# Attention that transposes the scores before the exponential, takes every fourth query row as a tile, and sums the weights by columns of ones

## The chip, the core and the metric

The kernel runs on one core of one Trainium2 chip. The time is the device time of one execution in microseconds: 3637.33 us in the median of three runs (3631.33 to 3641.29). Engines are named as in the profile: PE multiplies matrices (PEld is its weight load), DVE, ACT and POOL do element work, SP only starts transfers. Sixteen DMA engines move data between the chip's memory (HBM) and SBUF; SP's transfers go through the hardware queue q1, POOL's through the software queue q0.

## The reference

The attention is that of 16 batches of 512 rows of 256 numbers, with 16 heads of 16 numbers each, and a relative-position term on both sides:

```python
scores = jnp.einsum('bhqd,bhkd->bhqk', q, k)
dist_idx = pos_l - pos_r + M - 1
pos_emb = dist_emb[dist_idx]
rel_q = jnp.einsum('bhld,lrd->bhlr', q, pos_emb)
rel_k = jnp.einsum('bhrd,lrd->bhlr', k, pos_emb)
scores = (scores + rel_q + rel_k) / jnp.sqrt(jnp.asarray(D, scores.dtype))
probs = jax.nn.softmax(scores, axis=-1)
ctx = jnp.einsum('bhqk,bhkd->bhqd', probs, v)
```

Around it stand a modulated layer norm, the projections, the output product and a mixture of 8 experts with 2 active.

## The kernel before, in words

`program` (near the end of the file) runs five stages one after the other, each a block in which every engine has its own written-out order: modulation, projections, distances, attention, experts. Only `attention` is touched.

The stage `distances` works out rel_q + rel_k for all 256 pairs of batch and head (called heads below) and writes them to HBM as `r_scratch`, 1 MB for each head, in blocks of 128 query rows l by 128 key rows. It loads `d_q` and `d_k` from POOL's queue to 48, 32 and 16 partitions at a time (L589).

The stage `attention` takes a head as four tiles of 128 query rows by 512 keys (TT = 4, tile L holds rows 128L to 128L+127). For one tile, PE makes the product q k (L893, a weight load of 128 columns of `qa`, `kb` moving), DVE adds the tile of r, multiplies by -0.25 and takes the row minimum in the same instruction (L977, `neg` and `low`), ACT takes the exponential with the row minimum as bias and sums it over the row (L1035, `e` and `total`), PE transposes `e` in four pieces (L903), and DVE (odd tiles, L985) or ACT (even tiles, L1042) copies the transposed weights from PSUM to `eT`. For each group of four heads PE multiplies `v` with `eT` (L914), DVE inverts the sums (L991), POOL spreads them (L820), PE transposes that (L924), ACT copies it to SBUF (L1048), DVE scales (L998), and POOL stores the context (L828).

The transfers: SP loads r, one transfer of 256 KB for each tile, into a ring of four heads (L860, `load_r`); a tile of the ring is loaded again when L977 has used it. `v` is loaded by SP for four heads at a time (L866). POOL loads `qa` and `kb` of a batch, which is 16 heads (L811, seven transfers to 48, 32 and 16 partitions, 3 MB in all), when the products of the batch before last are done.

Of the kernel before, what the change touches and what calls it, by code (L numbers as in the profile page):

```python
# [26 lines left out]
P = 128  # L27
# [692 lines left out]
def attention(nc, qf_d, ks_d, v_d, r_d, cT_d, nb=NB):  # L720
# [6 lines left out]
    with ctx:  # L727
# [13 lines left out]
        AHEAD = 2  # L741
        BANKS = 3
        SLOTS = 2 * H
        NH, NGR = nb * H, nb * H // GH
        BG = H // GH
        ident = sb("t_ident", [P, P])
        qa = sb("t_qa", [ROWS, 1, SLOTS, S], BF16)
# [3 lines left out]
        neg = sb("t_neg", [P, TT, S])  # L751
        low = sb("t_low", [P, 2, TT])
        e = sb("t_e", [P, 2, TT, S])
        total = sb("t_total", [P, 2, TT, GH])
        inv = sb("t_inv", [P, 2, TT, GH])
        wide = sb("t_wide", [P, TT * GH, CT])
        ones = sb("t_ones", [P, TT * GH])
        wideT = sb("t_wideT", [P, S])
        eT = sb("t_eT", [P, 2, GH, TT, TT, P])
        out = sb("t_out", [P, 2, S])  # L760
        tiny = sb("t_tiny", [P, 8])
        p_s = [ps(f"t_ps{i}", [P, S]) for i in range(BANKS)]
        p_t = [ps(f"t_pt{i}", [P, TT, P]) for i in range(BANKS)]
# [8 lines left out]
        r_loaded = [sem(f"t_r_loaded{i}") for i in range(RR * TT)]  # L772
        scored = sem("t_scored")
        added = sem("t_added")
        exped = sem("t_exped")
        turned = sem("t_turned")
        even_out = sem("t_even_out")
        odd_out = sem("t_odd_out")
        pc_zero = sem("t_pc_zero")
        weighed = sem("t_weighed")  # L780
        inverted = sem("t_inverted")
        widened = sem("t_widened")
        wide_turned = sem("t_wide_turned")
        wide_out = sem("t_wide_out")
        ctx_done = sem("t_ctx_done")
        ctx_stored = [sem(f"t_ctx_stored{i}") for i in range(2)]

        def bank(j, L):

            return (TT * j + L) % BANKS  # L790

        def since(j, L):

            i = TT * j + L
            return BANKS if i >= BANKS else next(k for k in range(1, 2 * BANKS) if (i - k) % (TT * U) % BANKS == i)

        with nc.Block() as block:
            @block.gpsimd
            def _(pool):
                nc.gpsimd.memset(ones[:], 1.0).then_inc(ident_zero, 1)  # L800
                nc.gpsimd.memset(ident[:], 0.0).then_inc(ident_zero, 1)
                pool.wait_ge(ident_zero, 2)
# [3 lines left out]
                def load(pair, u):  # L806
                    b = 2 * pair + u
                    g, b8 = b // GB, b % GB
                    for tensor, src, runs in ((qa, qf_d, A_RUNS), (kb, ks_d, B_RUNS)):
                        for row, stored, rows in runs:  # L810
                            pool.dma_start(tensor[row:row + rows, :, u * H:(u + 1) * H, :].rearrange("r n h w -> r n (h w)"),  # L811
                                           src[g, :, b8, stored:stored + rows, :, :].rearrange("n r h w -> r n (h w)")
                                           ).then_inc(batch_loaded[u], 16)

                def widen(G, par):

                    pool.wait_ge(inverted, G + 1)
                    later(pool, wide_turned, G)
                    narrow = inv[:, par].rearrange("p l j -> p (l j)").unsqueeze(2).to_broadcast([P, TT * GH, CT])
                    nc.gpsimd.tensor_tensor(wide[:], narrow, ones[:].unsqueeze(2).to_broadcast([P, TT * GH, CT]),  # L820
                                            ALU.mult).then_inc(widened, 1)

                def store(b, k):

                    pool.wait_ge(ctx_done, BG * b + k + 1)
                    for j in range(GH):
                        row = (GH * k + j) * D
                        pool.dma_start(cT_d[b, row:row + D, :], out[j * CT:j * CT + D, k % 2, :]  # L828
                                       ).then_inc(ctx_stored[k % 2], 16)

                def batch(pair, u, more=True):
                    b = 2 * pair + u
                    for k in range(BG):
                        if more or k + 1 < BG:
                            widen(BG * b + k + 1, (k + 1) % 2)
                        if more and k == BG - 1 and (not isinstance(pair, int) or b + 2 < nb):

                            pool.wait_ge(scored, TT * H * (b + 1))
                            load(pair + 1, u)
                        store(b, k)  # L840

                for u in range(2):
                    load(0, u)
                widen(0, 0)
                with pool.Fori(0, nb // 2 - 1) as pair:
                    for u in range(2):
                        batch(pair, u)
                for u in range(2):
                    batch(nb // 2 - 1, u, more=(u == 0))

                for par in range(2):
                    pool.wait_ge(ctx_stored[par], 16 * GH * NGR // 2)

            @block.sync
            def _(sp):
# [7 lines left out]
                def load_v(G, b, k):  # L863

                    later(sp, weighed, TT * (G - 1))
# [4 lines left out]
                def heads(g, b, half):  # L870

                    for j in range(U):
                        load_r(g, H * b + U * half + j, j)
                        if j % GH == GH - 1:
                            k = (U * half + j) // GH
                            load_v(BG * b + k, b, k)

                for half in range(2):
                    heads(0, 0, half)
                for g in range((nb + GB - 1) // GB):  # L880
                    with sp.Fori(max(1, g * GB), min((g + 1) * GB, nb)) as b:
                        for half in range(2):
                            heads(g, b, half)

            @block.tensor
            def _(pe):
                pe.wait_ge(ident_done, 1)
                pe.wait_ge(pc_zero, 1)

                def score(n, j, L, slot):  # L890

                    later(pe, added, TT * n + L - since(j, L) + 1)
                    nc.tensor.matmul(p_s[bank(j, L)][:], qa[:, 0, slot, L * P:(L + 1) * P], kb[:, :, slot, :],  # L893
                                     start=True, stop=True).then_inc(scored, 1)

                def turn(n, j, L):
                    t = TT * n + L

                    pe.wait_ge(exped, t + 1)
                    before = TT * j + L - since(j, L)  # L900
                    later(pe, (even_out, odd_out)[before % 2], TT // 2 * (n - j) + before // 2 + 1)
# [4 lines left out]
                def weigh(G, par, c, loads):  # L906
                    if c == 0:

                        pe.wait_ge(even_out, TT // 2 * GH * (G + 1))
                        pe.wait_ge(odd_out, TT // 2 * GH * (G + 1))  # L910
                        pe.wait_ge(v_loaded[par], 16 * loads)
                        later(pe, ctx_done, G)
                    for j in range(GH):
                        last = nc.tensor.matmul(p_c[j * CT:j * CT + D, :], vv[:, par, j, c, :],  # L914
                                                eT[:, par, j, c].rearrange("p l q -> p (l q)"),
# [3 lines left out]
                def turn_wide(G, L):  # L919
                    if L == 0:  # L920

                        pe.wait_ge(widened, G + 1)
                        later(pe, wide_out, G)
                    last = nc.tensor.transpose(p_i[:, L * P:(L + 1) * P],  # L924
# [693 lines left out]
```

## Time and profile before

| | |
|---|---|
| median of three runs | 3637.33 us |
| the profiled execution | 3640.87 us, its span 3639.3 us |
| mean granted clock of PE | 0.812 of full speed |
| busy: PE, DVE, ACT, POOL | 76%, 63%, 49%, 22% of the span |
| distances | about 366 to 1606 us |
| attention | about 1606 to 2870 us |
| HBM to and from the core | 848.79 MB, 233 GB/s over the span |

The page cuts the span into 40 slices of 91 us and gives the busy tenths of each engine, the granted clock and the bytes moved. A slice says that an engine was busy, not that it set the time; for that the waits are read. Attention is slices 18 to 31.

### The profile page before, as it was taken

To read this page: it belongs to the slowest core of one execution; us is meant where nothing else is said; L and a number is where in the kernel's file an instruction comes from. 1 tells how busy PE (TensorE), PEld (TensorE's weight loads), DVE (VectorE), ACT (ScalarE), POOL (GpSimd) and SP (SyncE) were. 2 spreads that over 40 slices of the span, in tenths; PEclk is the share of its full clock that TensorE was granted. 3 is DMA by queue.
4 is the path that set the end of the run, shared out by engine and by line. 5 is a ranking of instruction groups with operands and counts; after the bars stand their busy time and mean duration, and the time that the engine had idled before them with its cause. 6 is when DMAs were issued, how large, how long until landed. Compare 5 with 4: busy or idle time off the path is not lost. (4 is left out here: it accounts for less than half of the span.)

```text
span 3639.3 us, 69041 instructions
## 1 busy us (share of the span) xinstructions
PE 2756.1 (76%) x18124; PEld 1921.6 (53%) x18124; DVE 2294.1 (63%) x6133; ACT 1772.2 (49%) x3509; POOL 807.3 (22%) x907
## 2 busy tenths in 40 slices
PE   4665676776767767638878888878888688888887
PEld 2443576665766767635545555545555344444443
DVE  5664354554545545438877888878888666666664
ACT  2443453443534445318877888878888511111111
POOL 2442110111111111001211222212121224433334
PEclk7888575666766667659888999989999889999999
DMA  4999898979889799899999999999999711111110
GB/s 114 226 221 209 183 358 314 340 289 334 330 312 365 291 345 338 325 292 279 264 254 268 270 274 273 267 257 275 274 276 274 212 43 61 61 61 61 61 61 19
DMA packets 899306, 848.79 MB, mean 233 GB/s; under 512 B 236808, under 2 KB 809536, under 8 KB 864688
## 3 DMA queue, kind: packets, MB, share of 16 engines
q1 hardware_dynamic: 840112, 640.95, 60.2%
q0 software_dynamic: 59136, 207.14, 21.0%
q8 instruction: 28, 0.46, 0.1%
q14 instruction: 30, 0.25, 0.0%
HBM read 507.88 MB, written 340.05 MB: 233 GB/s over the span
## 5 line engine op out<-in xcount | busy, mean ns | idle before, releaser
L697 DVE TENSOR_TENSOR d_r<-d_pk,d_r 128x1024 f32<-128x1024 f32 x512 | 620.9, 1224 | 622.1 <-PE d_pk L654 487.9
L684 ACT ACTIVATE d_r<-d_pq 128x1024 f32<-128x1024 f32 x512 | 532.6, 1052 | 693.4 <-PE d_pq L643 686.9
L1035 ACT ACTIVATE t_e<-t_neg,t_low 128x512 f32<-128x512 f32 x1024 | 738.7, 734 | 231.5 <-DVE t_low L977 230.1
L643 PE MATMUL d_pq<-d_win,d_q 96*128 96x128 bf16 x4096 | 488.1, 278 | 303.1 <-DMA d_q<-q_chunks_scratch 283.4
L977 DVE CUSTOM_DVE_ANT_0 t_neg<-t_ps,t_r 128x512 f32<-128x512 f32 x1024 | 671.8, 687 | 28.4 <-issue 28.3
L903 PE MATMUL t_pt<-t_ident,t_e 128*128 128x128 f32 x4096 | 642.0, 280 | 1.5 <-DVE t_eT L985 0.6
L643 PEld LDWEIGHTS d_pq<-d_win,d_q 96*128 96x128 bf16 x4096 | 433.5, 193 | 327.8 <-issue 229.6
L893 PE MATMUL t_ps<-t_kb,t_qa 96*128 (+1 forms) x1024 | 405.0, 396 | 247.6 <-DVE t_low L977 182.5
L903 PEld LDWEIGHTS t_pt<-t_ident,t_e 128*128 128x128 f32 x4096 | 518.0, 145 | 110.9 <-ACT t_eT L1042 13.7
L654 PE MATMUL d_pk<-d_win,d_k 96*128 96x128 bf16 x4096 | 501.5, 288 | 76.6 <-DMA d_k<-k_chunks_scratch 45.1
L654 PEld LDWEIGHTS d_pk<-d_win,d_k 96*128 96x128 bf16 x4096 | 441.1, 187 | 105.0 <-DVE d_r L697 56.7
L1335 PE MATMUL e_pX<-e_we,e_h2T 128*128 128x512 f32 x1024 | 483.4, 623 | 0.8 <-DVE e_odd L1538 0.2
L985 DVE COPY t_eT<-t_pt 128x512 f32<-128x512 f32 x512 | 351.0, 686 | 2.4 <-PE t_pt L903 1.9
L893 PEld LDWEIGHTS t_ps<-t_kb,t_qa 96*128 (+1 forms) x1024 | 104.1, 102 | 436.6 <-issue 403.8
L1042 ACT ACTIVATE t_eT<-t_pt 128x512 f32<-128x512 f32 x512 | 307.3, 600 | 19.4 <-PE t_pt L903 19.3
L1335 PEld LDWEIGHTS e_pX<-e_we,e_h2T 128*128 128x128 f32 x1024 | 196.7, 198 | 227.3 <-issue 215.2
L914 PE MATMUL t_pc<-t_eT,t_v 128*16 128x512 f32 x2048 | 279.9, 620 | 0.9 <-DVE t_out L998 0.9
L820 POOL TENSOR_TENSOR t_wide<-t_inv,t_ones 128x512 f32<-128x512 f32 x64 | 66.7, 1042 | 787.3 <-DVE t_inv L991 787.3
L1035 ACT ACTIVATION_READ_ACCUMULATOR t_e<-t_neg,t_low 128x1 f32 x1024 | 215.3, 210 | 0.0
L596 POOL DMA_DIRECT2D d_win<-table_scratch x32 | 17.1, 533 | 841.3 <-PE d_pk L654 797.9
L976 DVE MEMSET t_tiny<- 128x1 f32 x1024 | 60.4, 59 | 226.7 <-DMA t_r<-r_scratch 114.2
L1530 DVE SCALAR_TENSOR_TENSOR e_even<-e_pX,e_mask,e_even 128x256 f32<-128x256 f32 x192 | 92.1, 480 | 169.6 <-ACT e_even L1405 101.7
(133 smaller groups left out, 2560.3 us busy)
## 6 DMA issues: line engine op xcount, KB each, us to landing
r_scratch<-d_r SPq DMA_DIRECT2D x256, 1024.0 KB, 18.4
t_r<-r_scratch SPq DMA_DIRECT2D x1024, 256.0 KB, 5.3
d_q<-q_chunks_scratch POOLq DMA_DIRECT2D x64, 768.0 KB, 16.0
d_q<-q_chunks_scratch POOLq DMA_DIRECT2D x64, 512.0 KB, 17.8
d_q<-q_chunks_scratch POOLq DMA_DIRECT2D x64, 256.0 KB, 19.6
t_kb<-k_chunks_scratch POOLq DMA_DIRECT2D x32, 512.0 KB, 20.3
q_chunks_scratch<-a_part SPq DMA_DIRECT2D x96, 128.0 KB, 3.6
q_rows_scratch<-a_part SPq DMA_DIRECT2D x96, 128.0 KB, 2.2
```

The lines of the kernel that those rows point to most:

```text
L643: last = nc.tensor.matmul(pq[n % 2][:, a, :], q[u][:, :, l % CW], rhs, start=True, stop=True)
L654: last = nc.tensor.matmul(pk[n % 2][:, a, :], k[u][:, :, c % CW], win[par][:, TB - 1 - c:2 * TB - 1 - c], start=True, stop=True)
L684: nc.scalar.activation(r[u][:, n * QL:(n + 1) * QL, :], pq[n % 2][:], ACT.Copy).then_inc(q_out, 1)
L697: nc.vector.tensor_tensor(part, pk[n % 2][:].rearrange("p r l -> p l r"), part, ALU.add).then_inc(k_added, 1)
L893: nc.tensor.matmul(p_s[bank(j, L)][:], qa[:, 0, slot, L * P:(L + 1) * P], kb[:, :, slot, :], start=True, stop=True).then_inc(scored, 1)
L903: last = nc.tensor.transpose(p_t[bank(j, L)][:, c, :], e[:, j % 2, L, c * P:(c + 1) * P], ident[:])
L914: last = nc.tensor.matmul(p_c[j * CT:j * CT + D, :], vv[:, par, j, c, :], eT[:, par, j, c].rearrange("p l q -> p (l q)"), start=(c == 0), ...
L977: nc.vector.tensor_tensor_reduce(out=neg[:, L, :], in0=p_s[bank(j, L)][:], in1=r[:, j % RR, L].rearrange("p c r -> p (c r)"), scale=-0.25, ...
L985: nc.vector.tensor_copy(eT[:, j // GH, j % GH, :, L, :], p_t[bank(j, L)][:]).then_inc(odd_out, 1)
L1035: nc.scalar.activation(e[:, j % 2, L, :], neg[:, L, :], ACT.Exp, bias=low[:, j % 2, L:L + 1], scale=-1.0, accum_out=total[:, j // GH, L, j ...
L1042: nc.scalar.activation(eT[:, j // GH, j % GH, :, L, :], p_t[bank(j, L)][:], ACT.Copy).then_inc(even_out, 1)
L1335: last = nc.tensor.matmul(pX[n][:], h2T[:, u, k, t * P:(t + 1) * P], we[:, k, n * 2 * E:(n + 1) * 2 * E], start=(k == 0), stop=(k == KC - 1))
```

## The change

Tile t of a head is now made of the query rows t, t+4, t+8, ... (every fourth), so that partition p holds the rows 4p to 4p+3 of a head. One partition's piece of r for one block of keys is then 2 KB without a gap in HBM, instead of four of 512 bytes. `load_r` brings a head in four transfers of 256 KB, as before, but each of them goes to 32 partitions and holds all four tiles (L875), where one went to 128 partitions and held one tile. A head of the ring is loaded again when all its four tiles are used.

The row minimum is subtracted in place: of tiles 0 and 1 by POOL, of tiles 2 and 3 by ACT. PE then transposes the scores, two tiles to a pair of PSUM banks, and ACT takes the exponential of both out of PSUM straight to `eT`, once for 128x1024 elements. DVE and ACT no longer copy transposed tiles. The sums are made by PE: `vx` holds `v` and 16 columns of ones, so the product has 32 rows for a head, and one of them, the sum, is picked by four small products with `pick`. The banks for the scores are two instead of three, and the weight load of the scores reads every fourth column. Loads of `qa` and `kb` and stores of the context move from POOL's queue to SP's.

```diff
+        vx = sb("t_vx", [P, 2, GH, TT, 2, D])
-        r = sb("t_r", [P, RR, TT, NT, TB])
+        r = sb("t_r", [P, RR, NT, TT, TB])
...
+                def subtract(n, j, t):
+
+                    pool.wait_ge(added, TT * n + t + 1)
+                    nc.gpsimd.tensor_scalar(neg[:, j % RING, t, :], neg[:, j % RING, t, :],
+                                            low[:, j % RING, t:t + 1], None, ALU.subtract).then_inc(pool_sub, 1)
...
                 def load_r(g, n, j):
-                    for L in range(TT):
-
-                        later(sp, added, TT * (n - RR) + L + 1)
-                        sp.dma_start(r[:, j % RR, L], r_d[g][L, :, n - g * P, 0:TB * TB].rearrange("c (l r) -> l c r", r=TB)
-                                     ).then_inc(r_loaded[j % RR * TT + L], 16)
...
+                    later(sp, added, TT * (n - RR + 1))
+                    for lc in range(NT):
+                        src = r_d[g][lc, :, n - g * P, 0:TB * TB].rearrange("c (p x) -> p c x", x=TT * TB)
+                        sp.dma_start(r[lc * P // NT:(lc + 1) * P // NT, j % RR].rearrange("p c t r -> p c (t r)"), src
+                                     ).then_inc(r_loaded[j % RR], 16)
...
+                    for j in range(H):
+                        load_r(g, H * b + j, j)
+                        k = j // GH
+                        if j % GH == 0:
+                            load_v(b, k)
+                        if j % GH == 1 and (not fixed or BG * b + k >= 3):
+                            store(b + (k - 3) // BG, (k - 3) % BG)
+                        if j == 4 and (not fixed or 1 <= b < nb - 1):
+                            nxt = pair + u
+                            load_next((b + 1) // GB if fixed else g, nxt, 1 - u)
...
+                def score(n, j, t):
+
+                    later(pe, added, TT * n + t - 1)
+                    lhs = qa[:, 0, n % SLOTS, :].rearrange("r (p t) -> r t p", t=TT)[:, t, :]
...
+                    if t < 2:
+                        pe.wait_ge(pool_sub, 2 * n + t + 1)
+                    else:
+                        pe.wait_ge(act_sub, 2 * n + t - 1)
+                    if t % 2 == 0:
+                        later(pe, exped, 2 * n + t // 2 - 1)
                     for c in range(TT):
-                        last = nc.tensor.transpose(p_t[bank(j, L)][:, c, :], e[:, j % 2, L, c * P:(c + 1) * P], ident[:])
+                        last = nc.tensor.transpose(p_t[t // 2][:, t % 2, c, :],
+                                                   neg[:, j % RING, t, c * P:(c + 1) * P], ident[:])
                     last.then_inc(turned, 1)
...
+                def sums(G, par):
+
+                    pe.wait_ge(emptied, G + 1)
+                    later(pe, scaled, G)
+                    for t in range(TT):
+                        last = nc.tensor.matmul(p_i[:, t * GH:(t + 1) * GH], cs[:, par, t * P:(t + 1) * P], pick[:],
+                                                start=True, stop=True)
+                    last.then_inc(summed, 1)
...
+                    nc.vector.tensor_tensor_reduce(out=neg[:, j % RING, t, :].rearrange("p (c r) -> p c r", r=TB),
+                                                   in0=p_s[t % 2][:].rearrange("p (c r) -> p c r", r=TB),
+                                                   in1=r[:, j % RR, :, t, :], scale=-0.25,
                                                    scalar=3.0e38, op0=ALU.add, op1=ALU.min,
-                                                   accum_out=low[:, j % 2, L:L + 1]).then_inc(added, 1)
-
-                def empty(n, j, L, G):
-
-                    dve.wait_ge(turned, TT * n + L + 1)
-                    later(dve, weighed, TT * (G - 1))
-                    nc.vector.tensor_copy(eT[:, j // GH, j % GH, :, L, :], p_t[bank(j, L)][:]).then_inc(odd_out, 1)
...
+                    nc.scalar.activation(neg[:, j % RING, t, :], neg[:, j % RING, t, :], ACT.Identity,
+                                         bias=low[:, j % RING, t:t + 1], scale=-1.0).then_inc(act_sub, 1)
...
+                    nc.scalar.activation(to, p_t[half][:], ACT.Exp, scale=(1.0 if half else -1.0)).then_inc(exped, 1)
```

In SP's queue, from the start of the stage, the rows before are these; "128x4x128" is partitions, key blocks and numbers in a run.

```order
L860 DMA t_r<-r_scratch 128x4x128 x16
L866 DMA t_v<-v_scratch 128x256
L860 DMA t_r<-r_scratch 128x4x128 [waits t_added] x16
L866 DMA t_v<-v_scratch 128x256
L860 DMA t_r<-r_scratch 128x4x128 [waits t_added] x16
```

After, in the same queue at the fifth and sixth head of batch 1, L866 is the load of the next batch's `qa` and `kb`, L891 a store of the context:

```order
L875 DMA t_r<-r_scratch 32x4x512 [waits t_added]
L875 DMA t_r<-r_scratch 32x4x512 x3
L882 DMA t_v<-v_scratch 128x256 [waits t_v_copied]
L866 DMA t_qa<-q_rows_scratch 48x8192 [waits t_scored]
L866 DMA t_qa<-q_rows_scratch 32x8192
L866 DMA t_qa<-q_rows_scratch 16x8192
L866 DMA t_kb<-k_chunks_scratch 16x8x1024 x2
L866 DMA t_kb<-k_chunks_scratch 32x8x1024 x2
L875 DMA t_r<-r_scratch 32x4x512 [waits t_added]
L875 DMA t_r<-r_scratch 32x4x512 x3
L891 DMA ctx_scratch<-t_out 16x512 [waits t_scaled]
```

The loads of r change shape, and the batch load now stands between the loads of r of two heads in one queue.

On ACT, in the steady order of heads before:

```order
L1042 ACTIVATE t_eT<-t_pt 128x4x128 [waits t_turned]
L1035 ACTIVATE t_e,t_total<-t_neg,t_low 128x512 [waits t_turned,t_added] x2
L1042 ACTIVATE t_eT<-t_pt 128x4x128 [waits t_turned]
L1035 ACTIVATE t_e,t_total<-t_neg,t_low 128x512 [waits t_turned,t_added] x2
L1042 ACTIVATE t_eT<-t_pt 128x4x128 [waits t_turned]
```

and after, where L1064 subtracts and L1074 is the exponential:

```order
L1064 ACTIVATE t_neg<-t_neg,t_low 128x512 [waits t_added]
L1074 ACTIVATE t_eT<-t_pt 128x2x4x128 [waits t_turned]
L1064 ACTIVATE t_neg<-t_neg,t_low 128x512 [waits t_added]
L1074 ACTIVATE t_eT<-t_pt 128x2x4x128 [waits t_turned]
L1080 ACTIVATE t_cs<-t_pc 128x512 [waits t_weighed]
```

A head is six instructions with four row sums before, and four without them now.

## Rows read from the trace of the kernel before

**Rows 1.** The page: busy tenths and GB/s in 40 slices.
```profile
PE   4665676776767767638878888878888688888887
PEclk7888575666766667659888999989999889999999
DMA  4999898979889799899999999999999711111110
GB/s 114 226 221 209 183 358 314 340 289 334 330 312 365 291 345 338 325 292 279 264 254 268 270 274 273 267 257 275 274 276 274 212 43 61 61 61 61 61 61 19
```

**Rows 2.** Waits of SP, 1632 to 2870: us in total, times, longest.
```profile
SPq L866 <- PE t_pc L914: 20.7, 22, 1.9
SPq L860 <- DVE t_low L977: 19.2, 32, 1.8
```

**Rows 3.** Waits of all engines, 1632 to 2870, same columns.
```profile
DVE t_tiny L976 <- DMA t_r<-r_scratch: 114.2, 24, 14.7
```

**Rows 4.** Timeline of SP, one batch: start, duration, transfers issued.
```profile
2031.73 13.49 SPq L860 DMA_DIRECT2D t_r<-r_scratch  x16
...
2047.30 32.90 SPq L860 DMA_DIRECT2D t_r<-r_scratch  x16
```

**Rows 5.** Transfers issued 2070 to 2120: count, size, us to landing.
```profile
t_r<-r_scratch SPq DMA_DIRECT2D x55, 256.0 KB, 5.2
```

**Rows 6.** Windows: length, busy PE, PEld, DVE, ACT, POOL, clock, DMA share, GB/s.
```profile
1606.00:2854.00 1248.00, 1022.83 (x7266) 632.10 (x7266) 990.98 (x3664) 997.73 (x2587) 248.83 (x422) 0.90 1.14 268
2000.00:2050.00 50.00, 49.90 (x376) 31.24 (x374) 49.95 (x187) 49.68 (x131) 14.38 (x25) 1.00 1.20 294
2050.00:2070.00 20.00, 6.73 (x51) 4.43 (x47) 6.28 (x25) 7.33 (x19) 0.54 (x2) 0.79 1.01 179
1990.00:1998.00 8.00, 7.38 (x34) 4.32 (x35) 5.46 (x21) 5.07 (x13) 1.04 (x1) 0.57 1.20 292
```

**Rows 7.** Instructions from 2000 to 2050: count, busy us, mean ns.
```profile
L977 DVE CUSTOM_DVE_ANT_0 t_neg<-t_ps,t_r 128x512 f32<-128x512 f32 x52 | 34.0, 687 | 0.0
```

**Rows 8.** Windows with POOL's transfers alone: 128 partitions, then 16 to 48.
```profile
58.00:60.00 2.00, 2.00 (x5) 0.76 (x4) 0.00 (x0) 1.08 (x2) 0.00 (x0) 0.99 0.93 311
366.00:400.00 34.00, 18.11 (x144) 15.46 (x144) 0.79 (x1) 15.86 (x16) 11.06 (x20) 0.50 0.99 160
```

**Rows 9.** Their packets, the first for 58 to 60, the second for 366 to 400.
```profile
q0 software_dynamic: 168, 0.62, 93.3%
q0 software_dynamic: 1507, 5.42, 99.0%
```

**Rows 10.** POOL's timeline, first loads of distances (48, then 32 partitions).
```profile
366.03 0.66 POOL L589 DMA_DIRECT2D d_q<-q_chunks_scratch  x1
366.89 2.86 POOL L589 DMA_DIRECT2D d_q<-q_chunks_scratch  x5 [0.20 <-issue]
```

**Rows 11.** Those two transfers: size, us from issue to landing.
```profile
d_q<-q_chunks_scratch POOLq DMA_DIRECT2D x1, 768.0 KB, 8.2
d_q<-q_chunks_scratch POOLq DMA_DIRECT2D x1, 512.0 KB, 10.0
```

**Rows 12.** The page's costliest groups: count, busy us, mean ns.
```profile
L684 ACT ACTIVATE d_r<-d_pq 128x1024 f32<-128x1024 f32 x512 | 532.6, 1052 | 693.4 <-PE d_pq L643 686.9
L643 PEld LDWEIGHTS d_pq<-d_win,d_q 96*128 96x128 bf16 x4096 | 433.5, 193 | 327.8 <-issue 229.6
L985 DVE COPY t_eT<-t_pt 128x512 f32<-128x512 f32 x512 | 351.0, 686 | 2.4 <-PE t_pt L903 1.9
L893 PEld LDWEIGHTS t_ps<-t_kb,t_qa 96*128 (+1 forms) x1024 | 104.1, 102 | 436.6 <-issue 403.8
L1042 ACT ACTIVATE t_eT<-t_pt 128x512 f32<-128x512 f32 x512 | 307.3, 600 | 19.4 <-PE t_pt L903 19.3
L820 POOL TENSOR_TENSOR t_wide<-t_inv,t_ones 128x512 f32<-128x512 f32 x64 | 66.7, 1042 | 787.3 <-DVE t_inv L991 787.3
```

**Rows 13.** Instructions of the attention stage, 1590 to 2910, same columns.
```profile
L924 PE MATMUL t_pi<-t_ident,t_wide 128*128 128x128 f32 x256 | 73.0, 287 | 0.0
```

More of the change, by code:

```diff
@@ new lines, in head @@
+                def head(step, j):
+                    n = U * step + j
+                    fixed = isinstance(n, int)
+                    if not fixed or n < NH:
+                        for t in range(2):
+                            subtract(n, j, t)
+                    if j % GH == 0 and (not fixed or 2 * GH <= n):
+                        widen(2 * step + j // GH - 2)
+                    if j % GH == 1 and (not fixed or n < NH):
+                        copy_v(step, j // GH)
+                for n in range(NH + GH + 1):
+                    head(n // U, n % U)
@@ L815, in widen @@
[L815 to L829, printed above, removed]
@@ L844, in _ @@
[L844 to L855, printed above, removed]
[L856 to L865 removed]
+                            sp.dma_start(tensor[row:row + rows, :, u * H:(u + 1) * H, :].rearrange("r n h w -> r n (h w)"),
+                                         src[g, :, b8, stored:stored + rows, :, :].rearrange("n r h w -> r n (h w)")
+                                         ).then_inc(batch_loaded[u], 16)
@@ L868, in load_v, with store @@
                                  ).then_inc(v_loaded[k % 2], 16)
[L870 to L883, printed above, removed]
+                def store(b, k):
+                    sp.wait_ge(scaled, BG * b + k + 1)
+                    for j in range(GH):
+                        row = (GH * k + j) * D
+                        sp.dma_start(cT_d[b, row:row + D, :], out[j * CT:j * CT + D, k % 2, :]
+                                     ).then_inc(ctx_stored[k % 2], 16)
@@ new lines, in _ @@
+                for b in range(2):
+                    load(b)
+                for g in range(NG):
+                    first, last = g * GB // 2, (g + 1) * GB // 2 - 1
+                    for u in range(2):
+                        batch(g, first, u)
+                    with sp.Fori(first + 1, last) as pair:
+                        for u in range(2):
+                            batch(g, pair, u)
+                    for u in range(2):
+                        batch(g, last, u)
+                for k in range(BG - 3, BG):
+                    store(nb - 1, k)
@@ L885, in _ @@
+                for par in range(2):
+                    sp.wait_ge(ctx_stored[par], STORE * NGR // 2)
             @block.tensor
             def _(pe):
[L887 to L893, printed above, removed]
-                                     start=True, stop=True).then_inc(scored, 1)
@@ L929, in head, with widen @@
+                def widen(G):
+                    pe.wait_ge(widened, G + 1)
+                    for t in range(TT):
+                        last = nc.tensor.transpose(p_i[:, t * P:(t + 1) * P],
+                                                   wide[:, t * GH:(t + 1) * GH, :].rearrange("p j w -> p (j w)"), ident[:])
+                    last.then_inc(spread, 1)
                 def head(step, j):
@@ L1016, in _ @@
-                for step in range(2):
-                    for j in range(U):
-                        head(step, j)
-                with dve.Fori(2, NH // U) as step:
-                    for j in range(U):
-                        head(step, j)
-                for j in range(GH + 2):
-                    head(NH // U, j)
+                            add(n, j, t, step)
+                        G = 2 * step + k // GT - 2
+                        if k % GT == 1 and (not fixed or 0 <= G < NGR):
+                            invert(G)
```

271 lines of the change are left out of this document (133 added, 138 removed).

## The prediction

> **What bounds the kernel now.** First the page in 40 slices [rows 1]: in the slices of attention (18 to 31) PE stands at 7 or 8 tenths, while the DMA engines stand at 9 in every slice, at 254 to 279 GB/s once the stage runs. No engine is full, the transfers are. Second, the waits of SP [rows 2]: in 1238 us it waits 19.2 us for a free tile of the ring (L860, for DVE) and 20.7 us for L866. A queue bounded by the ring would wait there most of the time; this one always has a transfer to start, and what holds it is the transfers before. Third, whose wait it becomes: DVE stands 114.2 us before L976 for r [rows 3], in stops of up to 14.7 us.
>
> The timeline of SP gives the shape of a batch [rows 4]: sixteen loads of r are issued in 13.5 us, but the sixteen during which POOL loads `qa` and `kb` take 32.9 us, 19.4 us more. The steady rate is 55 loads in 50 us [rows 5], 0.909 us each with `v` and the context among them. A batch is then 64 x 0.909 + 19.4 = 77.6 us, and sixteen are 1241 us, against 1248 us from the first load of r to the last, the first line of [rows 6]. So the sum of the transfers accounts for the stage.
>
> The engines come close behind. Where r flows, 2000 to 2050, PE, DVE and ACT are each busy for 49.7 to 50.0 of 50 us at full clock [rows 6], and 52 tiles pass [rows 7]: 0.96 us a tile, 3.85 us a head, 61.5 us for a batch. The other 16 us of each batch are stops. This says what the change can win at most: with engines of no cost the transfers would still take 1241 us. The work on DVE and ACT is only worth something if the transfers get faster too.
>
> **The change, part by part.**
>
> Engines. DVE loses 512 copies of 686 ns; it is left with 1024 adds of 687 ns plus the small ones, under 3 us a head. ACT loses 1024 exponentials, their row sums and 512 copies, and gets 512 subtractions (between 600 ns, a copy of 128x512, and the 734 ns or so of a longer one) and 512 exponentials of 128x1024 (1052 ns, L684) [rows 12]: 2 x (0.60 to 0.73) + 2 x 1.05, about 3.4 to 3.6 us a head. POOL gets 512 subtractions; the nearest row is its spread of 128x512, 1042 ns [rows 12]. At that price 2.1 us a head, and with the spread and the copy of `v` shared by four heads under 2.7 us. It would need 1.8 us apiece to reach the 3.85 of now, which would be visible only where r keeps up. PE keeps its 4096 transposes and 1024 products. Its weight load reads every fourth column: 102 ns now, and 193 ns is the row for a load with gaps (L643) [rows 12], at most 4 x 0.09 = 0.36 us a head if nothing covers it. The products with `pick` are 256, dearer than nothing and no dearer than the 256 transposes of 287 ns [rows 13]: 73 us over 256 heads, 0.29 us each. So PE comes to between 3.85 and 4.5 us a head. I take 4.1. All engines stay under what the loads of r cost below, so they are entered at nothing; the cover is the wait for r, and without it PE is the bound (the first rival).
>
> Waits. `turn` now waits for POOL or ACT and for the exponential one half head back, where it had a bank in three. Behind it in PE's queue stand the next score and, through it, DVE's next add. There is a whole head between a subtraction and its transpose, so I enter nothing; if wrong it costs up to an exponential, 1.05 us a head, still below the bound.
>
> The loads of r. Same bytes, same count of 1024, but each lands in 32 partitions instead of 128. No load of r is like that now; those of POOL show the effect. Where only POOL's transfers run, those to 128 partitions (a_x, a_mod) move 311 GB/s at a DMA share of 0.93; those of `d_q` and `d_k` to 48, 32 and 16 partitions move 160 GB/s at a share of 0.99 [rows 8]. The engines are as busy and half as fast. Per packet: 16 x 2 x 0.933 / 168 = 178 ns for 3.7 KB against 16 x 34 x 0.99 / 1507 = 357 ns for 3.6 KB [rows 9]. Same queue, same size, twice the time. One transfer of exactly 32 partitions can be taken alone: the 768 KB issued at 366.03 lands 8.2 us later, at 374.2, and the 512 KB issued at 366.89 lands at 376.9 [rows 10, 11], so 512 KB take 2.7 us, 194 GB/s. That is with other transfers queued behind it, so alternating partitions did not help them overlap.
>
> The Trainium skill, SBUF — State Buffer, "Door 1: The DMA port swizzle", says that partitions 0 to 31 reach only 8 of the 16 ports (0 to 63 no more), with 189 GB/s measured at 1 MiB and 218 as the limit. The trace agrees as far as its 194 GB/s goes; by 218 the price below would be 4.81 us a head and the whole 3951 us.
>
> Price of a head of r: from below 311 GB/s, 3.37 us (no effect of partitions); from above 160 GB/s, 6.55 us (the mix with 16 partitions in it). I take 200 GB/s, next to the one row of this shape, a little above it since the first transfer there may have lagged: 1.049 MB / 200 = 5.24 us.
>
> Batch load and stores. The 3 MB of `qa` and `kb` go to the same partitions as before, now through SP's queue between two heads of r: the same 19.4 us, which DVE cannot hide since the ring is empty when loads bound the stage. Moving it to another queue changes the order, not the work; bounds are 12 us (3.1 MB at 268 GB/s) and 23 us. Stores of context (16 of 32 KB) and `v` were inside the 0.909 us; I add 2 us for a batch, as they now stand in line.
>
> Sum. 16 x 5.24 + 19.4 + 2 = 105.2 us a batch, 1684 us for sixteen, 436 us over the 1248 of now. On the profiled execution's 3641 us (4 us above the median of the runs, inside their spread) that is 4077; I say 4080. Its own range: at 160 GB/s and 3 us of stores 127 us a batch, but the row of this very shape is much nearer, so I cut at 167 GB/s (half of 311 / 0.93), 6.28 us a head, 122 us a batch and 4346; at 218 as worked out, about 3950.
>
> **Rivals.**
>
> *The loads of r escape the narrow partitions (12%).* For it: the slow rows are POOL's software queue, r comes by SP's hardware queue, and its runs grow from 512 bytes to 2 KB. Against it: the two rows of 128 and of fewer partitions are both software. Then a head of r costs 3.37 us at 311 GB/s or 2.93 at the 358 GB/s of the page's best slice [rows 1]; batch 54 or 47 plus 19.4 and 2: 75 or 68 us. PE at 4.1 us a head needs 66, so loads still bound. 1205 or 1094 us, 3598 down to 3487, middle 3545. It decides from 290 GB/s on, where r costs what it does now; below that the kernel is slower. The Trainium skill, DMA: Bandwidth & Descriptors, "Why small descriptors are slow", counts a fixed 3 cycles for each packet, which at 2 KB instead of 512 bytes gives a gain of some 13% and speaks for this rival; the trace agrees in direction, with 311 GB/s for packets of 3.7 KB against 294 for runs of 512 bytes, both at 128 partitions [rows 6, 8].
>
> *The two halves overlap (12%).* The four loads of a head go in turn to partitions 0 to 31, 32 to 63, 64 to 95, 96 to 127. If DMA engines drift apart, one may write low partitions while another writes high ones. Taking 250 GB/s: 4.19 us, 88.5 us a batch, 1416 us, 3809 us in all. Against it: the mix at 366 to 400 went to changing partitions too and stayed at 160 GB/s [rows 8].
>
> *PE's clock falls (6%).* Right after a stop the granted clock is 0.57 with PE busy 7.4 of 8 us, the last line of [rows 6], and in distances, slices 4 to 16, it is 0.5 to 0.7 with PE at 6 or 7 tenths [rows 1]; its two levels are 1.2 and 2.4 GHz. If waits for r kept PE at the lower, a head would cost up to 8.2 us, 131 us a batch, 2100 us, 4490 in all. Against it: a PE that falls behind has no idle time, and full stretches hold 1.0. From 0.8 of the clock on (4.1 / 5.24) it does not decide.
>
> **How the numbers follow.** 70% for the forecast, 12, 12 and 6 for the rivals. The likeliest gives 4080, own range 3950 to 4346. Overall I leave out the fast rival (12), a bit of the overlap and half of the slow clock: 3700 to 4370. Within 0.3% (11 us) is about what a measurement here cannot tell from no change. Faster 0.12, same 0.02 (r near 290 GB/s), slower 0.86.
>
> **What would show it.** Right: attention about 1680 us long, DMA busy tenths at 9 and GB/s near 200 in its slices, DVE waiting for t_r more than anything else, DVE busy under 60% in the stage, a load of r at 1.3 us from one to the next, SP waiting almost nowhere. For the rivals: GB/s over 290 and PE full; or 230 to 260 GB/s; or clock near 0.5 with PE full. The forecast is wrong if SP's queue waits for L977's successor, or if a 256 KB load of r follows another in under 1 us.

## The result, and the profile after

The changed kernel takes 3931.18 us (median of four runs, 3887.0 to 3933.91) against 3634.62 us: the ratio is 1.0785, with a 95% interval of 1.0707 to 1.0863. It is slower, by 297 us. The profiled execution took 3933.91 us; its span is 3932.4 us, 293 us longer than before. Its busy tenths and GB/s, as in [rows 1]:

```profile
PE   4774777677767768277777777777777859888888
DMA  4999889888898898999999999999999931111210
GB/s 121 222 226 186 258 321 347 313 327 325 313 367 302 321 368 315 235 210 237 222 218 208 214 217 224 224 224 216 203 211 215 220 122 57 57 56 57 77 63 18
```

The DMA engines are full as before, but they move 203 to 237 GB/s in the slices of attention, where it was 254 to 279. PE fell from 8 tenths to 7. The stages ahead end where they did (attention begins at 1606 us before and at 1604 now), and the experts take the same time. The adds of DVE, the first and last of which bracket the stage, ran from 1632.4 to 2864.8 before and run from 1649.8 to 3166.1 now, 1516 us instead of 1232. Those 284 us and the 17 us of later start (`qa` and `kb` of two batches now stand ahead of r in SP's queue, and the first load of r is issued at 1612.8 instead of 1606.1) are 301 us; 8 us come back after the last add.

The windows of the changed kernel, with the columns of [rows 6]; the second is a steady stretch, the third a stop, the fourth a stretch of another kind:

```profile
1606.00:3190.00 1584.00, 1155.00 (x7937) 749.44 (x7937) 775.35 (x3208) 857.32 (x1090) 852.66 (x642) 0.86 1.04 213
2066.00:2111.00 45.00, 41.24 (x277) 26.28 (x276) 26.76 (x111) 29.17 (x37) 29.41 (x22) 0.89 1.07 216
2034.00:2050.00 16.00, 0.16 (x2) 0.00 (x0) 0.00 (x0) 0.65 (x2) 0.00 (x0) 0.60 1.03 168
1980.00:1996.00 16.00, 16.00 (x121) 10.54 (x122) 11.68 (x48) 12.46 (x17) 12.56 (x9) 1.00 1.07 272
```

216 GB/s with the DMA engines at a share of 1.07, against 294 at 1.20 [rows 6]. The loads of r issued from 2066 to 2111, as in [rows 5]:

```profile
t_r<-r_scratch SPq DMA_DIRECT2D x35, 256.0 KB, 13.0
```

35 in 45 us are 1.29 us each, against 0.91 us. At 1980 to 1996, in another batch, the same loads ran at 272 GB/s; so the rate is not fixed. Whole batches differ too. These two windows go from one batch load in SP's queue to the next:

```profile
1926.80:2015.30 88.50, 68.53 (x489) 44.06 (x488) 47.93 (x198) 52.36 (x68) 52.11 (x40) 0.88 1.04 232
2015.30:2118.20 102.90, 76.09 (x502) 49.06 (x500) 48.91 (x201) 53.63 (x68) 53.57 (x41) 0.82 1.07 207
```

One batch takes 88.5 us, the next 102.9. The experiments take this up.

The waits read differently from what the prediction asked for. SP's own and DVE's, from 1632 to 3190:

```profile
SPq L875 <- DVE t_low L1025: 478.2, 194, 5.8
DVE t_tiny L1024 <- issue: 318.1, 37, 22.5
DVE t_neg L1025 <- issue: 217.2, 228, 4.6
DVE t_tiny L1024 <- PE t_ps L933: 119.0, 153, 2.7
DVE t_tiny L1024 <- DMA t_r<-r_scratch: 107.1, 24, 67.9
```

SP now waits 478 us for a free head of the ring (19.2 before, [rows 2]). Read alone, this says that the engines hold the loads up. But SP issues four loads at once when a head is used up and then waits, while up to three heads are still under way: a load of r lands 11.3 us after its issue in the median (5.3 before). A waiting SP is not a waiting DMA engine: the share of the DMA engines in the stage is 1.04. And of DVE's 761 us of idle time in these rows the profile puts 535 under "issue", where it names neither an engine nor a transfer; only 107 carry the name of r, 68 of them at the start.

The engines' part, with the columns of [rows 12]:

```profile
L818 POOL TENSOR_SCALAR t_neg<-t_neg,t_low 128x512 f32<-128x512 f32 x512 | 794.5, 1563 | 710.1 <-DVE t_low L1025 710.1
L933 PEld LDWEIGHTS t_ps<-t_kb,t_qa 96*128 (+1 forms) x1024 | 119.5, 117 | 711.0 <-issue 641.1 <-DVE t_low L1025 65.6
L967 PE MATMUL t_pi<-t_pick,t_cs 128*128 128x4 f32 x512 | 61.2, 243 | 0.7 <-ACT t_cs L1080 0.7
```

The relief is there: ACT is busy 857 us in the stage (998 before), DVE 775 (991), though the stage is longer. It bought no time.

### The profile page after: what moved, and what is told of

It reads as the page before. It is cut to its first block and busy times, and to the rows that moved or that the text cites. A ratio compares the mean times of both kernels' runs of the same rounds, so it can differ in the third digit from the quotient of the medians.

```text
span 3932.4 us, 62492 instructions
## 1 busy us (share of the span) xinstructions
PE 2869.9 (73%) x18636; PEld 2028.9 (52%) x18636; DVE 2068.1 (53%) x5620; ACT 1614.6 (41%) x1973; POOL 1402.5 (36%) x1117
## 5 line engine op out<-in xcount | busy, mean ns | idle before, releaser
L818 POOL TENSOR_SCALAR t_neg<-t_neg,t_low 128x512 f32<-128x512 f32 x512 | 794.5, 1563 | 710.1 <-DVE t_low L1025 710.1
L1074 ACT ACTIVATE t_eT<-t_pt 128x1024 f32<-128x1024 f32 x512 | 524.5, 1025 | 663.9 <-PE t_pt L945 663.8
L933 PE MATMUL t_ps<-t_kb,t_qa 96*128 (+1 forms) x1024 | 421.8, 412 | 440.8 <-DVE t_low L1025 384.5
L945 PE MATMUL t_pt<-t_ident,t_neg 128*128 128x128 f32 x4096 | 656.1, 285 | 0.2
L945 PEld LDWEIGHTS t_pt<-t_ident,t_neg 128*128 128x128 f32 x4096 | 547.1, 149 | 86.7 <-issue 13.4
L933 PEld LDWEIGHTS t_ps<-t_kb,t_qa 96*128 (+1 forms) x1024 | 119.5, 117 | 711.0 <-issue 641.1
L1064 ACT ACTIVATE t_neg<-t_neg,t_low 128x512 f32<-128x512 f32 x512 | 366.4, 716 | 89.6 <-DVE t_low L1025 89.6
L956 PE MATMUL t_pc<-t_eT,t_vx 128*32 128x512 f32 x2048 | 284.6, 630 | 0.7 <-ACT t_eT L1074 0.7
L1416 ACT ACTIVATE e_last_two<-e_pX,e_mask 128x256 f32<-128x256 f32 x128 | 53.6, 469 | 297.2 <-PE e_pX L1359 297.2
L589 POOL DMA_DIRECT2D d_q<-q_chunks_scratch x192 | 112.0, 589 | 95.6 <-PE d_pq L643 87.0
## 6 DMA issues: line engine op xcount, KB each, us to landing
t_r<-r_scratch SPq DMA_DIRECT2D x1024, 256.0 KB, 11.3
d_q<-q_chunks_scratch POOLq DMA_DIRECT2D x64, 256.0 KB, 19.2
```

Source lines behind the costliest of these rows:

```text
L818: nc.gpsimd.tensor_scalar(neg[:, j % RING, t, :], neg[:, j % RING, t, :], low[:, j % RING, t:t + 1], None, ALU.subtract).then_inc(pool_sub, 1)
L933: nc.tensor.matmul(p_s[t % 2][:], lhs, kb[:, :, n % SLOTS, :], start=True, stop=True).then_inc(scored, 1)
L945: last = nc.tensor.transpose(p_t[t // 2][:, t % 2, c, :], neg[:, j % RING, t, c * P:(c + 1) * P], ident[:])
L956: last = nc.tensor.matmul(p_c[j * CT:(j + 1) * CT, :], vx[:, par, j, c].rearrange("p o d -> p (o d)"), eT[:, par, j, c].rearrange("p t q - ...
L1064: nc.scalar.activation(neg[:, j % RING, t, :], neg[:, j % RING, t, :], ACT.Identity, bias=low[:, j % RING, t:t + 1], scale=-1.0).then_inc( ...
L1074: nc.scalar.activation(to, p_t[half][:], ACT.Exp, scale=(1.0 if half else -1.0)).then_inc(exped, 1)
```

## The experiments

### Wide loads in the changed kernel

`r` is laid out in HBM so that one load of 256 KB reaches all 128 partitions in runs of 2 KB. The stores of `distances` keep their runs of 8 KB. Nothing else is touched. The diff shows the loads; the addresses of the stores follow the layout.

```diff
-                    for lc in range(NT):
-                        src = r_d[g][lc, :, n - g * P, 0:TB * TB].rearrange("c (p x) -> p c x", x=TT * TB)
-                        sp.dma_start(r[lc * P // NT:(lc + 1) * P // NT, j % RR].rearrange("p c t r -> p c (t r)"), src
+                    for c in range(NT):
+                        src = r_d[g][c, n - g * P, 0:NT * TB * TB].rearrange("(p x) -> p x", x=TT * TB)
+                        sp.dma_start(r[:, j % RR, c].rearrange("p t r -> p (t r)"), src
```

> The changed kernel with r laid out in HBM as (key block, head, query row), so that one load of r is 256 KB to all 128 partitions in runs of 2 KB, where it was 256 KB to 32 partitions in runs of 2 KB; the engines' programs are the same. Theory A (the number of partitions a load reaches sets its time): a load falls from the 1.29 us of the steady stretch (35 in 45 us) to 0.75 to 0.90 us, a batch to 64 x 0.80 + 19.4 = 71 us or what PE needs, and the time to about 3530 us (3480 to 3620). Theory B (the ring by whole heads, the waits between POOL, ACT and PE, or POOL's subtraction of 1.56 us set the pace): stays at 3880 to 3940 us.

Measured: 3690.60 us, 1.0128 of the kernel before (1.0111 to 1.0145). 241 us of the 297 are gone by the shape of a load and the layout in HBM that goes with it, so B falls. It was not the 3530 us expected, nor within the 3480 to 3620. The windows say why:

```profile
1992.00:2000.00 8.00, 7.80 (x46) 5.01 (x47) 4.85 (x20) 3.27 (x4) 5.49 (x5) 0.77 1.06 385
2020.00:2046.00 26.00, 25.61 (x194) 17.66 (x192) 19.24 (x81) 21.47 (x29) 21.35 (x16) 1.00 0.81 260
2062.00:2066.00 4.00, 0.00 (x0) 0.00 (x0) 0.00 (x0) 0.52 (x1) 0.00 (x0) 0.74 1.08 136
```

After a stop r comes at 385 GB/s (292 in a like stretch of 8 us of the kernel before, [rows 6]), then PE is full and the DMA engines are at 0.81: the transfers are no bound there. But each batch still stops while `qa` and `kb` arrive.

### Narrow loads in the kernel before

```diff
-                    for L in range(TT):
-                        later(sp, added, TT * (n - RR) + L + 1)
-                        sp.dma_start(r[:, j % RR, L], r_d[g][L, :, n - g * P, 0:TB * TB].rearrange("c (l r) -> l c r", r=TB)
+                    later(sp, added, TT * (n - RR + 1))
+                    for w in range(4):
+                        src = r_d[g][:, :, n - g * P, w * 32 * TB:(w + 1) * 32 * TB].rearrange("L c (l r) -> l (L c) r", r=TB)
+                        sp.dma_start(r[w * 32:(w + 1) * 32, j % RR].rearrange("p L c r -> p (L c) r"), src
```

> The kernel before with one edit: a head of r comes in four loads of 256 KB to 32 partitions each (runs of 512 bytes as before), and a head of the ring is loaded again when all its four tiles are used. Theory A: the same loss as the change, 97 to 102 us a batch instead of 77.6, 3940 to 4030 us. Theory B (the engines' new order is what costs): within 30 us of 3634 us, or little more for the coarser ring.

Measured: 3931.79 us, 1.0791 (1.0767 to 1.0814), with none of the change's edits on PE, ACT, POOL or DVE (DVE only waits once for a head's r instead of once a tile). The medians are within a microsecond of each other; that close is luck, as the runs go from 3920.94 to 3940.49 us here and from 3887.00 to 3933.91 there. Its adds run from 1649.2 to 3165.1 us; the change's from 1649.8 to 3166.1. Its steady stretch:

```profile
2000.00:2050.00 50.00, 42.62 (x284) 22.39 (x282) 37.49 (x138) 39.25 (x100) 6.10 (x10) 1.00 1.22 216
```

The profile names r as the cause of DVE's waits here, 461 us from 1632 to 3190 where the change has 107.

Again 216 GB/s, now in runs of 512 bytes. With the two kernels above this makes a table of four: 128 partitions give 294 GB/s in runs of 512 bytes and 385 in runs of 2 KB; 32 partitions give 216 in either. Longer runs pay only where the width is there. The 385 came with the other layout in HBM as well, and no run has the one without the other at 128 partitions.

### 64 partitions

```diff
-                    for c in range(NT):
-                        src = r_d[g][c, n - g * P, 0:NT * TB * TB].rearrange("(p x) -> p x", x=TT * TB)
-                        sp.dma_start(r[:, j % RR, c].rearrange("p t r -> p (t r)"), src
+                    for half in range(2):
+                        src = r_d[g][:, n - g * P, half * 2 * TB * TB:(half + 1) * 2 * TB * TB].rearrange("c (p x) -> p c x", x=TT * TB)
+                        sp.dma_start(r[half * 64:half * 64 + 64, j % RR].rearrange("p c t r -> p c (t r)"), src
```

> As wide_loads (the same layout of r in HBM), but a head of r comes in two loads of 512 KB to 64 partitions each instead of four of 256 KB to 128. Theory A1 (what counts is the number of ports, and 64 partitions reach no more of them than 32): as the change, 213 GB/s in the steady stretch and 3930 us (3890 to 3960). Theory A2 (the rate grows with the number of partitions): halfway between 213 and 386 GB/s, so that PE bounds between the stops, 3700 to 3780 us. Theory C (it was the layout of r in HBM, and not the width, that made wide_loads fast): near 3690 us.

Measured: 3925.26 us, 1.0808 (1.0767 to 1.0849), with runs from 3876.63 to 3947.40 us, as wide a spread as the change has (3887.00 to 3933.91) or wider. A1 holds: twice the partitions, no gain clear of that spread, and nothing like the 3700 to 3780 us of A2. A steady stretch of it:

```profile
2600.00:2640.00 40.00, 35.10 (x248) 23.07 (x248) 23.25 (x96) 25.70 (x33) 26.59 (x20) 0.96 1.07 218
```

The layout in HBM is that of the wide loads here, so the layout alone does not make loads fast.

The Trainium skill, SBUF — State Buffer, "Door 1: The DMA port swizzle", gives partitions 0 to 63 the same 8 of 16 ports as 0 to 31, with a limit of about 218 GB/s. The steady stretches agree with it, at 216 and 218 GB/s; the stretch of 272 in the changed kernel is above it, and the next experiment bears on that.

### The order of the four loads

```diff
-                    for lc in range(NT):
+                    for lc in (0, 2, 1, 3):
```

> The changed kernel with the four loads of a head in the order of partitions 0-31, 64-95, 32-63, 96-127. Theory A with DMA engines in step: no change, 3930 us within 0.5%, since at each moment only half of the ports is written. Theory A with drift (the stretches at 257 to 272 GB/s are loads to the two halves overlapping): now a drift of one load is enough, so more overlap, 3700 to 3850 us. Theory B: no change.

Measured: 3834.02 us, 1.0536 (1.0493 to 1.0579), 97 us faster than the change by an order alone. If the partitions of a load alone set its time, the order would not matter; the gain fits loads to the two halves that overlap in part when they follow one another directly. The stretch from 2000 to 2040 ran at 213 GB/s and that from 2300 to 2340 at 239; from about the first add to the last the mean is 232, against 216 in the change:

```profile
1650.00:3070.00 1420.00, 1106.51 (x7826) 719.56 (x7830) 772.92 (x3184) 843.37 (x1078) 848.71 (x636) 0.89 1.06 232
```

That DMA engines write both halves at once was not seen directly, and why it would be so in one batch and not in another was not found.

### The engines' own pace, without r

Only the first four heads of r are loaded, in the changed kernel and in the kernel before; the adds then use what is in the ring.

```diff
+                    if not isinstance(n, int) or n >= RR:
+                        return
```

> The changed kernel with only the first four heads of r loaded; all later heads use what is in the ring (the values of r are then those of other heads). Shows the engines' own pace. Theory A: PE near 4.1 us a head sets it, 66 us a batch, attention about 1080 us, 3450 us in all. Theory B: a head stays near 4.9 us, 3850 us or more.

> The kernel before with only the first four heads of r loaded; later heads use what is in the ring. Shows the pace of the old engines' order. From the full stretch of the trace (52 tiles in 50 us): 3.85 us a head, 3.63 ms less 1248 plus 1010 us = 3390 us. If it comes near 3495 us like the changed kernel without r, both orders have the same pace.

Measured: 3494.90 us and 3564.03 us, one run each. The windows from the first add to the last, first of the changed kernel, then of the one before:

```profile
1656.00:2731.00 1075.00, 1058.71 (x7860) 693.73 (x7861) 777.50 (x3194) 841.07 (x1082) 851.36 (x638) 1.00 0.33 59
```

```profile
1632.00:2793.00 1161.00, 1023.10 (x7346) 643.47 (x7345) 1001.15 (x3700) 1007.41 (x2615) 242.01 (x409) 0.94 0.31 57
```

In the changed kernel PE is busy 1059 of 1075 us: the pace is 4.20 us a head, and theory A's 4.1 was near. The second number missed its forecast of 3390 us by 174: the old order is not held by its engines' pace there but by a stop in each batch, in which PE waits at the start of a step for `kb`:

```profile
PE t_ps L893 <- DMA t_kb<-k_chunks_scratch: 119.9, 14, 9.2
```

So the change does bring something, hidden by the narrow loads: its batch load is issued when the first head of a batch has been added, on SP, where POOL issued it after the sums of the first four heads (its `widen` stands ahead). PE asks for it at the eighth head, and no longer waits: its one wait for `kb` in that run is the 46.0 us ahead of the stage's first product.

### PE's wait moved, in the kernel before

```diff
-                    pe.wait_ge(batch_loaded[0], BATCH * ((step + 1) // (SLOTS // U) + 1))
-                    pe.wait_ge(batch_loaded[1], BATCH * ((step + 1 + H // U) // (SLOTS // U)))
                     for j in range(U):
+                        if j == U - 1:
+                            pe.wait_ge(batch_loaded[0], BATCH * ((step + 1) // (SLOTS // U) + 1))
+                            pe.wait_ge(batch_loaded[1], BATCH * ((step + 1 + H // U) // (SLOTS // U)))
```

> The kernel before with one edit: in the loop PE waits for qa and kb of the next eight heads just before the last head of the step instead of at its start. In before_no_r this early wait stops PE for about 7 us a batch. If the same wait was part of the 14 to 16 us stop of a batch in the kernel before: up to 16 x 7 = 112 us less, 3525 to 3600 us. If the missing r alone made that stop (the transfers' sum of 77.6 us a batch stays): within 10 us of 3637 us.

Measured: 3640.23 us, ratio 1.0000 (0.9985 to 1.0015). With r to load, the wait lies under the missing r. That agrees with the prediction's sum of the transfers, 77.6 us a batch, but does not prove it: the last experiment finds a second bound at the same height.

### Spreading the batch load

In the changed kernel with wide loads, one of the seven loads of `qa` and `kb` after each of heads 4 to 10, and PE's wait moved as above:

```diff
-                        if j == 4 and (not fixed or 1 <= b < nb - 1):
+                        if 4 <= j < 11 and (not fixed or 1 <= b < nb - 1):
                             nxt = pair + u
-                            load_next((b + 1) // GB if fixed else g, nxt, 1 - u)
+                            load_next((b + 1) // GB if fixed else g, nxt, 1 - u, j - 4)
```

> wide_loads with the seven loads of qa and kb issued one each after the loads of r of heads 4 to 10 of a batch instead of all after head 4, and PE's wait for them moved to the last head before they are used. If the stops of 14 us a batch in wide_loads are the burst and nothing else, they go, and PE's 4.20 us a head bounds: 16 x 67.2 = 1075 us instead of 1271, 3495 us (3480 to 3560). If they are the loads' own price (the sum of the transfers), a batch stays at 64 x 0.68 + 19.4 = 63 us and does not show under PE; only if the narrow loads slow those of r beside them does it stay above 3600 us.

Measured: 3606.82 us, 0.9928 (0.9900 to 0.9956). The stops of 14 us are gone, 84 us of the 195 expected are won: adds from 1644.9 to 2831.2 are 74.1 us a batch, against PE's 67.2. From 1640 to 2700 DVE still waits 141.3 us for r in 28 stops, 66 us of them at the start. The loads of `qa` and `kb` keep their narrow shape, and a time above 3600 us was the expectation's sign that they slow r behind them; that share was not separated.

### The old engines' order with wide loads

```diff
-                    nc.tensor.matmul(p_s[bank(j, L)][:], qa[:, 0, slot, L * P:(L + 1) * P], kb[:, :, slot, :],
+                    lhs = qa[:, 0, slot, :].rearrange("r (p t) -> r t p", t=TT)[:, L, :]
+                    nc.tensor.matmul(p_s[bank(j, L)][:], lhs, kb[:, :, slot, :],
...
+                                                   in1=r[:, j % RR, :, L, :], scale=-0.25,
```

The diff shows the weight load of the score and the add; r is loaded and laid out as in the wide loads above. First with the burst of `qa` and `kb` as it was:

> old_wide_spread without the spreading: the old engines' order with wide loads of r, qa and kb loaded in one burst on POOL's queue, and PE's wait at the start of the step. If the burst is what the spreading removed: a batch of 61.5 us plus a stop of 12 to 15 us, 3600 to 3640 us, against the 3521 us of old_wide_spread. If wide loads alone give the gain: near 3521 us.

then spread in three portions, on POOL's queue, with PE's wait moved:

> The kernel before (its engines' programs, weights transposed) with tiles of every fourth row, the loads of r to 128 partitions in runs of 2 KB, and the loads of qa and kb issued in three portions (POOL's queue). If the engines' pace of before is 3.85 us a head and transfers are no bound any more: 16 x 61.5 = 985 us of attention instead of 1248, 3380 us (3370 to 3470), faster than both kernels. If the engines' new order is better than the old one once r flows, this is slower than wide_spread.

Measured: 3634.90 us, 0.9981 (0.9966 to 0.9997), for the first; 3520.72 us, 0.9684 (0.9667 to 0.9702), for the second, the fastest kernel of the study. The windows from first to last add of the second:

```profile
1631.00:2750.00 1119.00, 1036.09 (x7347) 642.14 (x7346) 1018.83 (x3703) 1011.71 (x2615) 240.31 (x409) 0.97 0.99 295
```

Wide loads alone win 7 us at most, since the stop of each batch stays (from 1640 to 2700, PE waits 148.8 us for `kb` and DVE 123.6 us for r in the first of these two). Between the stops the engines set the pace there, with the DMA engines at 0.84:

```profile
2100.00:2120.00 20.00, 19.70 (x148) 12.46 (x146) 19.94 (x73) 19.66 (x53) 3.05 (x5) 1.00 0.84 296
```

This bears on the kernel before as well. At 385 GB/s a load of r takes 0.68 us instead of 0.909, which makes the sum of the transfers 64 x 0.68 + 19.4 = 63 us a batch instead of 77.6. If that sum alone had bounded the kernel before, wide loads would have won some 230 us. They won 7: a batch still takes 77.2 us (adds from 1634.5 to 2869.7 us), 61.5 at the engines' pace and some 16 in the stop while the batch load arrives. The kernel before then stands on two bounds of the same height. That is inferred from this run; wide loads with PE's wait moved and the burst kept were not run.

Wide loads, the spreading and PE's later wait together win about 115 us; the spreading and the wait were not run apart. The batch is 69.9 us where the engines' pace of 3.85 us a head would allow 61.5, so the forecast of 3380 us was too good by 141. Beside it the changed order, with wide loads and its own spreading on SP's queue, is slower by 86 us. Its PE carries more, 4.20 us a head against 3.85; as the two kernels also spread the batch load differently, the 86 us are not split.

## Why the prediction was right, and where it was off

*The bound.* "The transfers are" holds for the changed kernel and is half of the truth for the one before. Narrowing the loads cost 8%, and the engines' new order cost or won nothing measurable while r bounded, as the change and the narrow loads in the kernel before show (3931.18 and 3931.79 us; the two also differ in run length and in the queue of the batch load). For the kernel before, the sum of 1241 us against 1248 was in part luck: cheaper loads of r won 7 us there and not 230, since the engines' pace and the stop of each batch give the same 77 us. The forecast of the change did not hang on this, as loads of 4.7 us a head and more stand above either bound.

*The loads of r.* The direction and the mechanism hold, and the price was mis-sized. The prediction took 200 GB/s, 5.24 us a head; steady stretches show 35 loads in 45 us, 5.14 us a head with `v` and the context in it, and the slowest batch shown above takes 102.9 us against the 105.2 of the sum; faster stretches (272 GB/s) and batches (88.5 us) bring the mean down. Adds of 1516 us are 94.8 us a batch; less 19.4 for the batch load that is 4.71 us a head, with stores and `v`, where the sum had 5.24 and 2 us a batch, together 5.36. 16 x 16 x (5.36 - 4.71) is 167 us too many, and the later start and the different ends of the two counts make 143 of it, the distance between 4077 and 3934. The measured time lies just below the forecast's own range, which begins at 3950, and inside the overall one. The row it went by (512 KB in 2.7 us) came from transfers between others of 48 and 16 partitions. The limit of 218 GB/s that the Trainium skill states in SBUF — State Buffer, "Door 1: The DMA port swizzle", came nearer. The prediction's 3951 us for it is a slip: 4.81 us a head with its own 19.4 and 2 us is 98.4 us a batch and 3967 us in all. The rival in which the halves overlap (250 GB/s, 3809 us) had a part of the truth: some stretches and batches ran faster than others, and the counter-argument to it, that changing partitions had not helped at 366 to 400 us, was too strong.

*The 2 us for stores and `v`.* Not separated; within the 167 us.

*The engines, entered at nothing.* Right for the sum. PE at 4.1 us a head measured 4.20. The weight load with every fourth column was bounded by 193 ns and takes 117. The subtraction on POOL was priced at 1042 ns by a row of another operation and takes 1563, half as much again; at 3.3 us a head with the rest it still lies under 4.20. The 256 products with `pick` come as 512 records of 243 ns that overlap and keep PE busy for 61.2 us in all, 0.96 us for four heads; 73 us was the bound.

*The batch load.* Its stop is there (2034 to 2050; DVE idle for up to 22.5 us at a time); its 19.4 us of transfers were taken over from before and not measured apart. That its earlier issue takes away a wait of PE was not foreseen; with the narrow loads it wins nothing, without r it shows.

*The markers.* Two of those named were wrong. SP "waiting almost nowhere" and "wrong if SP's queue waits for L977's successor": SP waits 478 us, and the bound is still the transfers, because a free head is asked for four loads at a time and little is issued ahead. And r shows as the cause of only 107 us of DVE's idle time, the rest is under "issue". The rate in GB/s and the interval from load to load were the markers that held.

*The fast rival.* It asked whether hardware-queue loads of 2 KB runs escape the narrow partitions. They don't: 216 GB/s at 32 partitions in either run length. Runs of 2 KB in the new layout are faster at 128 partitions, 385 against 294 GB/s or 31%. The prediction's estimate from the Trainium skill, DMA: Bandwidth & Descriptors, "Why small descriptors are slow", was 13%, so the measured gain is the bigger one.

*The clock.* It did not decide. It is 0.86 in the stage against 0.90 before, and 0.90 in the narrow loads in the kernel before, which takes the same time as the change. It reads 0.50 at the end of the stop and from 2056 to 2060, where PE is busy throughout, and 0.60 from 2090 to 2100, so the lower level is not confined to the stops.

## What to carry to other kernels

When a queue never waits for its ring and the DMA engines stand at 9 tenths, add up the transfers of one period before pricing any engine work: here 64 loads and one burst gave the stage to within 1%. Add up the engines' pace and the stops as well: here they gave the same number, and the transfers made cheaper by themselves won 7 us. Then look at which partitions a transfer reaches: runs four times as long, in a layout to match, came a third faster where all 128 are reached, and nothing where 32 are. A burst of narrow transfers beside them is the next thing to spread: wide loads alone gave 7 us on the kernel before, with the burst spread and PE's wait moved as well about 115.

## What the runs showed of the hardware

- Full DMA engines moved 294 GB/s to 128 partitions in runs of 512 bytes, 385 in runs of 2 KB (with another layout in HBM, over 8 us), and 216 to 32 partitions in both; 64 neighbouring partitions gave no more time back than 32 (3925 against 3931 us, within the spread of the runs).
- The rate of loads to 32 partitions is not fixed: 272 GB/s in a stretch of the changed kernel, 216 in another, and putting loads to the lower and upper half in turns won 97 us. Overlap of the two halves explains both; it is inferred from the rates.
- GpSimd's subtraction of one number per partition from 128x512 takes 1563 ns, its copy of the same size with a broadcast source 609 ns (L832 of the changed kernel), and its product of two broadcast operands 1042 ns [rows 12].
- An fp32 product of 4 columns behind a weight load of 128 comes as two records of 243 ns that overlap, and takes 239 ns of PE in the mean (61.2 us for 256).
